# A graph network on one core: comparisons split by lane, transposes and fronts moved ahead

## What is computed

```python
def _demo_layer(h, src, dst, deg_pos, inv_deg, Wg, Wl, Ws, b):
    g = h @ Wg
    neigh_mean = segment_sum(h[dst], src, n) * inv_deg[:, None]
    extra = neigh_mean @ Wl + h @ Ws
    return elu(g + deg_pos[:, None] * extra + b)
...
# last layer, node_i = src, node_j = dst and the reverse, and each node to itself
source_node_vec = segment_sum([x[node_i], stf], node_i) / max(cnt, 1)
neighbor_emb = [x[node_j], ef, et] @ W1.T + b1
out = [relu(segment_sum(neighbor_emb, node_i)), source_node_vec] @ W2.T + b2
x = layernorm(x + out)
```

## Time and profile before

| | us |
|---|---|
| median of 3 runs | 10247.38 (10235.4 to 10252.48) |
| profiled execution | 10235.93, of which the span of instructions 10234.1 |
| TensorE matmul, weight load busy | 6644.4, 5928.3 |
| VectorE busy | 6362.2 |
| ScalarE busy | 3417.6 |
| GpSimd busy | 5079.3 |

### The profile page before, as it was taken

The page is one execution under the profiler, slowest core; times in us unless marked ns, Lnnn a source line. Parts: engine busy times, 40 slices in busy tenths (PEclk is TensorE's granted clock), DMA queues, the critical chain, the costliest instruction groups (busy, mean ns, idle before and its releaser), DMA issues.

```text
span 10234.1 us, 185993 instructions
## 1 busy us (share of the span) xinstructions
PE 6644.4 (65%) x46642; PEld 5928.3 (58%) x46642; DVE 6362.2 (62%) x14404; ACT 3417.6 (33%) x8867; POOL 5079.3 (50%) x4833
## 2 busy tenths in 40 slices
PE   7899999800079997655556655566535566666665
PEld 6799999800079997554445554455524555445555
DVE  8899994300066665555666656666567666676656
ACT  0011110000067786333681116811149411681111
POOL 0047778877734445774017750077600577217750
PEclk5555555555589998887898877988869888898886
DMA  9987775566689998776597774977819877997770
GB/s 384 391 247 184 187 184 121 127 157 160 151 264 320 321 324 258 192 192 122 223 363 217 220 165 187 379 217 217 190 44 395 272 215 215 287 363 215 217 168 13
DMA packets 1567394, 2320.66 MB, mean 227 GB/s; under 512 B 974517, under 2 KB 1046057, under 8 KB 1567321
## 3 DMA queue, kind: packets, MB, share of 16 engines
q1 hardware_dynamic: 1227608, 1356.73, 39.2%
q0 software_dynamic: 292608, 911.36, 32.6%
q10 hardware_dynamic: 47104, 51.75, 2.3%
HBM read 1328.55 MB, written 986.78 MB: 226 GB/s over the span
## 4 chain that ended last, share of the span: by engine, by line
POOL 22%; issue 20%; DMA 18%; PE 16%; DVE 15%; ACT 6%; DVEq 1%; ACTq 1%; POOLq 0%; SPq 0%
POOL by_src L578 10%; DMA ring<-gathered,gidx 8%; POOL ring L649 8%; PE ps L759 6%; DMA gathered<-ring 4%; POOL ring L633 4%; PE ps L837 3%; DMA rows<-by_src,gidx 3%; ACT ring L1075 3%; DMA frows<-by_src 2%; ACT hring L1085 2%; PE ps L752 2%; DVE mask L1315 2%; DVE ohj L1225 2%; DVE prod L1303 2%
## 5 line engine op out<-in xcount | busy, mean ns | idle before, releaser
L649 POOL DMA_INDIRECT ring<-gathered,gidx x2176 | 2304.2, 1059 | 2847.0 <-DMA gathered<-ring 2112.2
L578 POOL DMA_INDIRECT by_src<-prow,ppos x1562 | 1710.1, 1095 | 1105.1 <-DMA ppos<-pos 632.5
L987 ACT COPY gidx<-move 128x4 int32 (+1 forms) x816 | 158.5, 197 | 3723.0 <-DMA ring<-gathered,gidx 2385.6
L1392 DVE TENSOR_REDUCE red<-ps 128x256 f32<-128x768 f32 x680 | 650.1, 956 | 1125.4 <-PE ps L837 914.1
L1471 DVE CAST ring<-ps 128x384 bf16<-128x384 f32 x2176 | 1107.3, 552 | 349.5 <-PE ps L752 308.6
L752 PE MATMUL ps<-hring,oht_g 128*128 128x192 bf16 x8704 | 907.7, 246 | 581.8 <-ACT ring L1075 182.9
L752 PEld LDWEIGHTS ps<-hring,oht_g 128*128 128x128 fp8e4 x8704 | 658.5, 97 | 831.0 <-issue 796.3
L1075 ACT CAST ring<-ps 128x384 bf16<-128x384 f32 x2176 | 1127.9, 520 | 11.5 <-PE ps L752 11.4
L759 PE MATMUL ps<-frows,hring 128*128 128x193 f32 x4352 | 1005.9, 384 | 160.9 <-DMA frows<-by_src 128.3
L759 PEld LDWEIGHTS ps<-frows,hring 128*128 128x128 f32 x4352 | 878.4, 231 | 181.4 <-DMA frows<-by_src 133.0
L717 PE MATMUL ps<-snap,oht_e 98*128 98x98 f32 x3130 | 956.2, 445 | 0.0
(11 more groups left out here) (228 smaller groups left out, 12270.2 us busy)
## 6 DMA issues: line engine op xcount, KB each, us to landing
gathered<-ring SPq DMA_DIRECT2D x544, 768.0 KB, 6.2
by_src<-zeros SPq DMA_DIRECT2D x34, 6272.0 KB, 46.3
frows<-by_src SPq DMA_DIRECT2D x544, 392.0 KB
oht_g<-oht SPq DMA_DIRECT2D x544, 256.0 KB, 6.1
gathered<-got SPq DMA_DIRECT2D x136, 776.0 KB
prow<-in_edge_attr_n SPq DMA_DIRECT2D x284, 352.0 KB
bc<-tidrow ACTq DMA_DIRECT2D x313, 160.0 KB
prow<-in_edge_attr SPq DMA_DIRECT2D x142, 352.0 KB
```

Of the source, the lines that this page charges most:

```text
L578: pool.indirect_dma_start(out=table, out_offset=bass.IndirectOffsetOnAxis(ap=ppos[:, s, j:j + 1], axis=0), in_=prow[:, s, j, :], in_offset ...
L649: pool.indirect_dma_start(out=ring[:, c, :], out_offset=None, in_=gb, in_offset=offsets(g, c % 4)).then_inc(q.got[c], 16)
L1392: return dve.tensor_reduce(red[:, u, :, 0:D], sums_of(bank)[:, :, 0:HW].rearrange("p b (a d) -> p b d a", d=D), AX.X, ALU.add)
```

## The change

Six things are changed; the values computed stay the same.

1. The mask of a rank step is made by five `tensor_scalar` instructions, one per lane, with `tid_f` as the scalar of each partition, instead of one `tensor_tensor` on `tid["s"]`. 
2. The comparison of a move group is made by four `tensor_scalar` instructions instead of one `tensor_tensor`.
3. In the pass by dst TensorE transposes block b+1 ahead of the feature sum of block b. `q.mm` now counts picks and `q.gmm` is gone; ScalarE waits for `q.mm` ahead of a block's `oht` (for `q.tr` only ahead of the first), and VectorE does `picked` of block b right after the addition of block b instead of one block later.
4. The feature sums of the later sums go round over four PSUM banks (4 to 7) instead of two.
5. In the dense layers VectorE's front is two groups ahead of its back, TensorE does the product of i and then the turn of i+2, and both wait for the buffers that this uses again.
6. In the last layer the first three instructions of `finish` become `middle_of`, which stands ahead of the front of the next group.

```diff
@@ pass by dst, TensorE
+                        if not (last and c == TURN - 1):
+                            pe.wait_ge(q.oh, b + 2)
+                            if not first or c > 0:
+                                pe.wait_ge(q.oht, b)
+                            turned(3 - u, oh[:, (c + 1) % 4])
-                        pe.wait_ge(q.oh, b + 1)
-                        if not first or c > 1:
-                            pe.wait_ge(q.oht, b - 1)
-                        turned(q, b, u, 2 + u, oh[:, c % 4])
                         pe.wait_ge(q.ohf, b + 1)
                         if not first or c > 1:
                             pe.wait_ge(q.add, b - 1)
-                        feature_sum(u, ohf[:, u], rows[:, c % 8]).then_inc(q.mm, 1)
+                        feature_sum(u, ohf[:, u], rows[:, c % 8])
...
-                        pick(4 + 2 * u, oht[:, c % 8, :], hring[:, c % 8, :]).then_inc(q.gmm, 1)
+                        pick(4 + 2 * u, oht[:, c % 8, :], hring[:, c % 8, :]).then_inc(q.mm, 1)
@@ sums, TensorE
-                        if q.f0 > 0 or not first or g > 1:
-                            pe.wait_ge(feat_add, f - 1)
-                        feature_sum(4 + u, fohf, frows[:, u]).then_inc(feat_mm, 1)
+                        if q.f0 > 0 or not first or g > 3:
+                            pe.wait_ge(feat_add, f - 3)
+                        feature_sum(4 + g, fohf, frows[:, u]).then_inc(feat_mm, 1)
@@ dense layer, TensorE
-                turn(0, 0)
-                with pe.Fori(0, NGROUPS // 2 - 1) as half:
+                for u in range(2):
+                    turn(u, u)
+                for u in range(2):
+                    product(u, u, u)
+                    turn(2 + u, u)
+                with pe.Fori(1, NGROUPS // 2 - 1) as half:
                     for u in range(2):
-                        turn(2 * half + (u + 1), 1 - u)
                         product(2 * half + u, u)
-                turn(NGROUPS - 1, 1)
-                product(NGROUPS - 2, 0)
-                product(NGROUPS - 1, 1)
+                        turn(2 * half + (u + 2), u)
+                for u in range(2):
+                    product(NGROUPS - 2 + u, u)
@@ pass by dst, ScalarE
-                        act.wait_ge(q.tr, b + 1)
+                        if first and c == 0:
+                            act.wait_ge(q.tr, 1)
+                        else:
+                            act.wait_ge(q.mm, b)
@@ dense layer, ScalarE
-                transposed(q, q.c0 + 1, 0, 0)
+                for u in range(2):
+                    transposed(q, q.c0 + u + 1, u, u)
                 with act.Fori(0, NGROUPS // 2 - 1) as half:
                     for u in range(2):
-                        transposed(q, 2 * half + (q.c0 + u + 2), 1 - u, 1 - u)
+                        act.wait_ge(q.mm, 2 * half + (q.c0 + u + 1))
+                        transposed(q, 2 * half + (q.c0 + u + 3), u, u)
                         group(2 * half + u, u)
@@ ranks, VectorE
-                dve.tensor_tensor(mask[:, u], bc[:, u, :].rearrange("p (l q) -> p l q", q=P),
-                                  tid["s"][:, bass.ds(n * LANES, LANES)].unsqueeze(2).to_broadcast([P, LANES, P]),
-                                  ALU.is_equal).then_inc(s_same, 1)
+                for l in range(LANES):
+                    ins = dve.tensor_scalar(mask[:, u, l, :], bc[:, u, l * P:(l + 1) * P],
+                                            tid_f[:, bass.ds(n * LANES + l, 1)], None, ALU.is_equal)
+                ins.then_inc(s_same, 1)
@@ moves, VectorE
-                    dve.tensor_tensor(
-                        cmp[0:T + 1, u], iota_row[0:T + 1, :].unsqueeze(1).to_broadcast([T + 1, 4, P]),
-                        thr[k][0:T + 1, bass.ds(j * 4, 4)].unsqueeze(2).to_broadcast([T + 1, 4, P]),
-                        ALU.is_ge).then_inc(s_cmp, 1)
+                    for c in range(4):
+                        ins = dve.tensor_scalar(cmp[0:T + 1, u, c, :], iota_row[0:T + 1, :],
+                                                thr[k][0:T + 1, bass.ds(j * 4 + c, 1)], None, ALU.is_ge)
+                    ins.then_inc(s_cmp, 1)
@@ pass by dst, VectorE
-                            if not first or c > 0:
-                                picked(b - 1, (c - 1) % TURN, first and c < 9)
                             dve.wait_ge(q.mm, b + 1)
...
                             dve.tensor_tensor(to, to, ps[:, c % 2, 0:FEAT], ALU.add).then_inc(q.add, 1)
+                            picked(b, c, first and c < 8)
@@ dense layer, VectorE (in the loop)
-                        front(2 * half + (u + 1), 1 - u)
+                        dve.wait_ge(q.tr, 2 * half + (q.c0 + u + 1))
+                        front(2 * half + (u + 2), u)
                         back(2 * half + u, u, half)
@@ last layer, VectorE (in the loop)
+                        middle_of(2 * half + u, u)
                         front(2 * half + (u + 1), 1 - u)
                         finish(2 * half + u, u)
```

More of the change, by code:

```diff
@@ L780, in body @@
                         pe.nop(nofuse=True)
-                        pick(4 + 2 * u, oht[:, c % 8, :], hring[:, c % 8, :]).then_inc(q.gmm, 1)
-                loop(pe, body)
+                        pick(4 + 2 * u, oht[:, c % 8, :], hring[:, c % 8, :]).then_inc(q.mm, 1)
+                pe.wait_ge(q.oh, 1)
+                turned(2, oh[:, 0]).then_inc(q.tr, 1)
+                body(0, True)
+                with pe.Fori(1, NI - 1) as i:
+                    body(i, False)
+                body(NI - 1, False, True)
             def wide_by_src(q):
@@ L992, in place, with whole @@
                     act.copy(loc[2][:, bass.ds(b * K, K)], rows[:, c % 8, :, LD]).then_inc(q.loc, 1)
-                def whole(b, c, first):
+                def whole(b, c):
                     act.wait_ge(q.oh, b + 1)
-                    if not first:
-                        act.wait_ge(q.mm, b - 1)
                     act.copy(ohf[:, c % 2], oh[:, c % 4].rearrange("p n k -> p k n")).then_inc(q.ohf, 1)
                 def picked(b, c, first):
-                    act.wait_ge(q.gmm, b + 1)
                     if not first and c % 4 == 0:
@@ L1021, in body @@
                         if not (last and c == TURN - 1):
-                            whole(b + 1, c + 1, first and c < 1)
+                            whole(b + 1, c + 1)
                         if c % 4 == 3 and not last:
@@ L1031, in wide_by_dst @@
                     place(b, b)
-                whole(0, 0, True)
+                whole(0, 0)
                 body(0, True)
@@ L1400, in picked @@
                 def picked(b, c, first):
-                    dve.wait_ge(q.gmm, b + 1)
                     if not first and c % 4 == 0:
@@ L1593, in back @@
                     assert step.n == per_back, (step.n, per_back)
-                front(0, 0)
                 for u in range(2):
-                    front(1 + u, 1 - u)
+                    front(u, u)
+                for u in range(2):
+                    dve.wait_ge(q.tr, q.c0 + u + 1)
+                    front(2 + u, u)
                     back(u, u, 0)
@@ L1638, in finish @@
                     dve.tensor_scalar(cat[:, :, 0:D], na, 0.0, None, ALU.max).then_inc(q.cat3, 1)
+                def finish(i, u):
+                    na, nb, nm, hs, ps = nas[u], nbs[u], nms[u], hss[u], ps_o[u]
+                    step = Steps(q.v, i, 10)
+                    step.n = 1
                     dve.wait_ge(q.cat3, i + 1)
```

24 lines of the change are left out of this document (13 added, 11 removed).

## The result

| | before | after |
|---|---|---|
| median, us | 10245.7 (10235.4 to 10252.5, 4 runs) | 9846.1 (9828.4 to 9864.9, 4 runs) |
| span of the profiled execution, us | 10234.1 | 9838.5 |

A forecast was written before the change was run, and what follows sets the result against it. A different resource bounds each stage: GpSimd's issues the scatter and sums, weight loads and DMA the pass by dst, VectorE's waits the dense and last layers. -149 - 30 - 152 - 59 = -390 us gave 9857 us, range 9790 to 9965.

The forecast's parts named there:

- Scatter: Indirect DMA issues on GpSimd: shorter VectorE instructions in ranks and moves take 118 issues from the tail, -149 us (0 to -213).
- The moves: Scatter issues while moves are computed: four short lanes give 1.29 us an issue, 360 issues instead of 277.
- the ranks: Scatter issues while ranks are computed: five mask lanes give 1.34 us an issue, 35 more by the ranks' end.
- the tail's cover: VectorE's 812 us idle in the scatter's tail hide ranks that end some 35 us later.
- rival 3: Scatter: tensor_scalars lock GpSimd out as long as they run; scatter grows by 241 us, 10297 us in all; chance 0.04.
- Rival 2: Scatter: lanes in a row hold GpSimd like one instruction, so the moves give nothing; 9962 us; chance 0.12.
- Pass by dst: Turns one block ahead give ScalarE's ohf more slack: -30 us (+10 to -68).
- rival 1: Pass by dst: DMA keeps its pace, so the new order gains nothing; 9887 us; chance 0.17.
- Dense layers: Fronts two groups ahead remove VectorE's 183 us wait for the product, less 31 us of new waits: -152 us (-110 to -183).
- the exponential's: Dense layers: ScalarE's copy delays the exponential, 10 us over 28 groups plus 13 us from table loads in the third layer.
- Last layer: Middle step before the next front: a group takes 15.35 us instead of 19.92, 13 groups, -59 us (-40 to -75).
- Banks and sums: Feature sums over four banks: TensorE's 28.7 us of waiting can go, but GpSimd paces the sums, so 0.

The follow-up runs named there:

- the run of the masks alone: Kernel before with only the rank mask compared in five lanes of 128 columns instead of one instruction of 640; long set: 11424.7 us, ratio 1.0044.
- ordinary set: Group of runs made beside the kernel before, in which that kernel takes 10246 to 10253 us.
- the last probe: Changed kernel with mask lanes in two kinds, moves half in one tensor_tensor and half in four, and unread VectorE work in the scatter's tail: 9991.1 us, ordinary set.
- eight in bf16: Changed kernel with the sums' one-hots of four blocks compared in eight tensor_tensor of 256 columns, the features' in two halves: 9729.4 us, ratio 0.9495.
- the sums with four pieces: Changed kernel with the sums' one-hots of four blocks compared in four tensor_tensor of 512 columns instead of one of 2048: 9698.6 us, ratio 0.9467.
- the long sets: Groups of runs in which the kernel before takes 11372, 11467 and 11374 us and ranks and moves end the scatter stage; reason unknown.

## Why the prediction was right, and where it wasn't

*Scatter.* Right in direction and mechanism, too small: -184 instead of -149. The moves gave 364 issues against 360 forecast. The mis-sized term is the ranks: 1.29 us an issue instead of 1.34, so by the moment at which the ranks of before ended 60 issues more instead of 35. With 87 more in the moves that is 147, and times 1.26 us it is 185. The forecast scaled an average over random starts. The trace has no random starts: three issues go round with each step of 3.87 us, one of them falls into L1237 and waits 0.07 us, the other two fall where nothing holds them (the reading of PSUM in L1315, a mask lane). The step grew to 3.87 us and the ranks ended 28 us later, as forecast (3.9 and 35). Where the tail's cover is missing this probably costs as much: 26 us in the run of the masks alone. No run has the masks alone in an ordinary set, so their share is read from the count of issues; the moves' share has the last probe behind it.

*What holds an issue.* The forecast's sentence, that an issue is held if it starts while VectorE runs a `tensor_tensor` on two SBUF tensors, named too little. L1320 in the earlier trace rows ran in mid-issue and so said nothing of a start inside a `tensor_scalar`; as evidence against rival 3 it was misread. The probe has 1.99 us an issue for both kinds. The number didn't suffer, because what decided it was that the pieces are short. Rival 2 was false for four lanes in f32 and true, for some issues, for eight in bf16.

Of the page "SBUF — State Buffer", section "Who interferes with whom", the Trainium skill's rule on 2-port `tensor_scalar` is borne out in that it stalls an issue (1.68 us instead of 0.96). The rule speaks of one instruction; that a row of them shuts GpSimd out, as rival 3 took it, is not so: 49 issues got through in 98 us beside 98 of them. No trace shows in which mode they ran. The inference that `tensor_tensor` does not stall descriptor generation is not borne out: 1.68 us as well. "GPSIMD Engine Reference", section "Key points", puts contention with both a 2-port mode and two SBUF inputs, which agrees. By rival 3 the kernel would have been 50 us slower than before; it was 400 faster.

*Pass by dst.* -23 for -30, `ohf` waited for 17.9 us instead of 41.6 (under 20 forecast), stage 1107 (1105). Right. DMA share went from 0.94 to 0.96, in part rival 1.

*Dense layers.* -158 for -152. The product's wait went (183 to 7.0 us; 8 forecast) and the exponential's came: 34.4 us in all instead of 17.3, +17 where 10 + 13 were forecast. In the first two layers the copy's delay cost 5 us (10 forecast), and in the third, with its table loads, 12 (13 forecast). 176 less 17 is 159, and 158 were measured. Right in every term; the exponential's was a little large.

*Last layer.* -46 for -59. The group of 15.35 us was put together from rows with TensorE partly at either clock. At a granted clock of 0.73 a group takes 14.65 to 14.92 us, at 0.50 it takes 18.15, and the mean of the changed kernel's 13 is 15.86. Before, when TensorE waited for VectorE in each group, they took 19.3 to 20.1 us. So one part of the miss is the clock: 13 groups of 15.86 us instead of 15.35, 7 us. The other is the factor 13: only 12 groups took some 19.9 us, and the last, with no front behind it, took 14.6 already before, 6 us in all.

*Banks and sums.* 0, as forecast.

*The total.* The span fell by 396 us where 390 were forecast, and the median is 11 us from the forecast. That is closer than the terms were, and so in part luck: the scatter gave 35 us and the dense layers 6 more than forecast, the last layer 13, the pass by dst 7 and the sums 14 less.

## What to carry over

Where an engine's DMA issues pace a stage, look at the single VectorE instruction that they start in: split it until an issue hardly feels a piece (here 128 f32 columns, or 512 bf16), for the two kinds tried here, and stop before the pieces are so short that they hold in a row (256 bf16). Count what the pieces cost on VectorE, and name the cover: masks and moves together gained 184 us where GpSimd ended the stage, and where ranks and moves did, neither gained anything and the masks probably cost some 26 us. And look for the next place at once: the same split of one more instruction was worth 147 us beyond the change.

## What the runs showed of the hardware that was not expected

- A long f32 `tensor_scalar` and a long f32 `tensor_tensor`, both 0.96 us, hold an indirect DMA's issue alike: 1.68 us instead of 0.96, once for each issue.
- What counts is the moment. In the sums with four pieces (bf16, 512 columns, each 0.41 us long and starting 0.33 us after the one before) an issue with 0.13 to 0.38 us left of the piece it started in waited that less 0.12 us. With 0.06 to 0.12 us left it didn't wait, and with less than 0.06 us left the next piece held it, for 0.21 to 0.27 us.
- bf16 `tensor_tensor` of 256 columns in a row held an issue for 0.71 us, the rest of the row, and did so nearly only to issues that started with 0.08 or 0.09 us of one left, to 158 of 373 of these; f32 lanes of 128 columns in a row didn't hold beyond one. Why the ones do and the others don't is open.
- In the long sets the same program took 11372 to 11467 us, 11% to 12% more. In the kernels with the ranks of before the pass by dst began 680 to 725 us later, since in the ranks TensorE at times started one instruction in 0.70 us; the four sums were 70 to 85 us longer each. The changes to order (pass by dst, dense layers, last layer) gained there as much or more; the two that spare GpSimd gained nothing.
